# A mixture-of-experts layer's row table: from one packed table to a region per expert

## The chip, the cores and the metric

One Trainium2 chip, one of its cores. The metric is the device time of one launch in microseconds. The core's engines are called PE (TensorE), DVE (VectorE), ACT (ScalarE), POOL (GpSimd) and SP (SyncE). SP and ACT issue plain DMAs; POOL issues the indirect ones, whose row addresses come from memory.

## The reference, cut to what matters

```python
x = L0_attn_x                                  # (8, 512, 256) float32: 4096 tokens
x = x + _L0_attn_ref(_layernorm(x), ...)       # only the first 16 rows of each of the 8 batches
                                               # attend (eff = 16); for all others only the bias ob is added
x = x + _L0_ffn_ref(_layernorm(x), ...)

# _L0_ffn_ref, for each token: E = 32 experts, 4 of them chosen
scores = sigmoid(tokens @ router_weight.T)     # groups of 8 experts; the best 2 of 4 groups stay,
topk_idx, topk_w = ...                         # of these the 4 best; weights scaled to a sum of 2.5
hidden_vals = silu(tokens @ gate_w[e].T) * (tokens @ up_w[e].T)     # I = 128
expert_out = hidden_vals @ down_w[e].T
mixed = sum over the 4 chosen of topk_w * expert_out
return mixed + shared                          # shared: two more experts, for every token
```

So the 128 rows that attend have their second-layer input only after three rounds of attention; the other 3968 rows have theirs at once.

## The kernel before

The tokens are 32 tiles of 128 rows. Tile 0 holds the attending rows (16 of each batch), tiles 1 to 31 all others. Everything is float32. Each engine's program is written out by hand, with semaphores between them; no scheduler moves anything.

**Stage 1, tiles 1 to 31 (0 to 57 us).** DVE adds `ob` and takes the statistics (`statistics`, groups of tiles in `GROUPS_OF_TILES`), ACT normalises (L572), PE turns the tile (L736), ACT keeps the turned tile (L577), PE makes the 32 logits of the router (L742), ACT the sigmoid (L581) in two halves.

**Stage 2, routing on DVE (41 to 89 us).** `route` (L1069 to L1122) finds the four experts of each token for one half of the tiles, two matmuls (L760, L767) count pairs per expert, and DVE makes from the counts of **all** tiles the place of each (token, expert) pair in one packed table of 128-row slots, `slots_dram`, in which each expert's rows begin where the expert before it ends (L1234 to L1267). The table is first filled with blank rows by four DMAs from SP (L398), 160 tiles of 128 rows.

**Stage 3, attention and the shared experts (88 to 220 us).** `ATT_STEPS` = 23 small steps alternate PE and DVE (`after_dve` and `from_pe`; ACT does some). Between them, by the list `UNITS_AT`, stand 48 units of the shared experts: 16 gate, 16 up and 16 down; 38 of them within the 23 steps, 10 behind. PE does its units of a step before it waits for DVE's part of that step. In the same time POOL scatters the normalised rows of tiles 1 to 31 to the table: four indirect DMAs of 128 rows for each tile (L535), each followed by a one-column memset on POOL (L538). ACT writes the rows that are scattered (`stage`, L598 and L600) in a ring of four tiles, and waits in `stage(n)` until tile n - 4 has landed. `STAGE_AT` says at which step each `stage(n)` stands, `ADD_AT` where DVE adds the shared result. Behind step 22, tile 0 is normalised, turned and routed (`route_parts(0, 1, 3)`).

**Stage 4, tile 0 through all experts (220 to 263 us).** `PLAN` holds 32 "dense" steps: the 128 rows of tile 0 go through every expert, weighted by `w0`, and PE sums in PSUM (L961).

**Stage 5, the table's tiles (263 to 483 us).** 134 "expert" steps (`FIXED`). SP loads 128 rows of the table (L425, ring of 16), PE turns them (L922), gate and up (L946), silu on ACT (L689), product on DVE (L1439), PE turns (L952), DVE copies (L1445), down (L970), ACT copies (L698), POOL scatters the 128 results to `pairs_dram` by an indirect DMA (L542). Parts behind `FIXED` run only if the table is longer (`used_parts`).

**Stage 6 (483 to 549 us).** For each of the tiles 1 to 31 SP loads the four result rows per token (L457), DVE adds them with their weights (L1477), SP stores.

For the inputs here the routing fills 133 tiles of the table with the pairs of tiles 1 to 31, and 136 with those of all 32 tiles, each expert rounded up to whole tiles (counted from the reference's choice of experts).

## Time and profile before

| | us |
|---|---|
| median of 3 runs | 551.88 (550.71 to 553.16) |
| the profiled execution | 550.75 |
| its span, first to last instruction | 549.0 |
| TensorE clock granted, mean of the span | 0.936 |
| first attention step on PE | 88.27 |
| dense steps begin | 219.74 |
| first expert step on a tile of the table | 264.88 |
| last expert step | 481.16 |

Times in the rows are microseconds from the span's start. A row of the timeline names the engine, the line of the kernel, the operation, what it writes and reads, and in brackets how long the engine had been idle and what released it. The clock is given as a share of full speed (2.4 GHz); half of it is the lower level, 1.2 GHz.

### The profile page before, as it was taken

The page shows a single profiled execution, that of the slowest core. Times are in us where ns is not written, and L with a number is a line of the kernel's source. Part 1 is how long each engine was busy: PE and PEld are TensorE (multiplying, and loading weights), DVE is VectorE, ACT ScalarE, POOL GpSimd, SP SyncE. Part 2 cuts the span into 40 slices and gives each one's busy share as a digit, 9 for nine tenths or more (in the row PEclk, how much of TensorE's full clock was granted, in tenths as well). Part 3 has the DMA queues.
Part 4 walks back from the last instruction along what each step waited for, and adds up shares of the span by engine and source line. Part 5 has one row for each costly group of instructions (what it writes and reads, how often), then busy time and mean ns, then how long its engine had stood idle before and what let it go on. Part 6 is the DMA issues. An engine that isn't in the chain of part 4 may idle for free.

```text
span 549.0 us, 8776 instructions
## 1 busy us (share of the span) xinstructions
PE 418.3 (76%) x2118; PEld 325.6 (59%) x2119; DVE 280.3 (51%) x997; ACT 240.5 (44%) x625; POOL 287.9 (52%) x421
## 2 busy tenths in 40 slices
PE   0699236898896976999999999999999999920000
PEld 0699114555453543888888888888888888810000
DVE  4967785764553434343366633223232322308997
ACT  0687501427644552422455555555555555510000
POOL 6430028886888888760166565656656565630000
PEclk9999998999998998999999999999999999985555
DMA  7999999532232373935055555455454454339996
GB/s 178 274 419 417 418 423 398 149 107 77 106 106 98 106 266 124 366 98 155 11 168 157 162 152 149 153 162 157 145 169 153 154 172 139 105 106 410 369 402 241
DMA packets 42549, 111.48 MB, mean 203 GB/s; under 512 B 7929, under 2 KB 25468, under 8 KB 38272
## 3 DMA queue, kind: packets, MB, share of 16 engines
q1 hardware_dynamic: 29824, 78.24, 41.5%
q0 software_dynamic: 12384, 32.59, 17.1%
q8 instruction: 23, 0.38, 0.3%
q14 instruction: 30, 0.25, 0.2%
q10 hardware_dynamic: 288, 0.03, 0.0%
HBM read 53.01 MB, written 59.13 MB: 204 GB/s over the span
## 4 chain that ended last, share of the span: by engine, by line
PE 53%; DVE 9%; ACT 2%; DMA 1%; issue 1%; SPq 0%; POOL 0%; POOLq 0%; ACTq 0%; DVEq 0%
PE two_banks L946 26%; PE two_banks L970 11%; DVE x_sb L1477 9%; PE two_banks L922 5%; PE two_banks L952 3%; PE two_banks L783 3%; PE two_banks L961 3%; PE two_banks L809 2%; DMA gu_w<-pairs_dram 1%; ACT L588 0%; ACT loopb L598 0%; DMA pairs_dram<-routing,loopb 0%; ACT routing L612 0%; PE two_banks L887 0%; PE two_banks L904 0%
## 5 line engine op out<-in xcount | busy, mean ns | idle before, releaser
L542 POOL DMA_INDIRECT pairs_dram<-routing,loopb x134 | 131.8, 984 | 112.0 <-issue 80.9
L535 POOL DMA_INDIRECT slots_dram<-loopb,slot_i x124 | 121.5, 979 | 70.6 <-DVEq L1267 41.8
L946 PE MATMUL two_banks<-gu_w,routing 128*128 x536 | 137.9, 380 | 0.0
L1439 DVE TENSOR_TENSOR routing<-routing,two_banks 128x128 f32<-128x128 f32 x134 | 38.6, 288 | 135.8 <-ACT routing L689 122.9
L946 PEld LDWEIGHTS two_banks<-gu_w,routing 128*128 128x128 f32 x536 | 91.5, 190 | 7.0
L970 PE MATMUL two_banks<-dn_w,routing 128*128 x268 | 80.0, 381 | 0.0
L684 ACT ACTIVATE routing<-two_banks 128x256 f32<-128x256 f32 x134 | 51.5, 384 | 64.9 <-PE two_banks L922 64.9
L783 PE MATMUL two_banks<-gu_w,sgu_w 128*128 128x512 f32 x128 | 64.8, 644 | 11.1 <-DMA sdn_w<-in_sh_down 5.5
L689 ACT ACTIVATE routing<-two_banks 128x128 f32<-128x128 f32 x166 | 46.1, 278 | 58.7 <-PE two_banks L946 58.7
L1477 DVE SCALAR_TENSOR_TENSOR x_sb<-gu_w,wts,x_sb 128x256 f32<-128x256 f32 x124 | 49.5, 480 | 12.7 <-DMA gu_w<-pairs_dram 12.6
L698 ACT ACTIVATE routing<-two_banks 128x256 f32<-128x256 f32 x134 | 50.6, 378 | 1.4 <-PE two_banks L970 1.3
L922 PE MATMUL two_banks<-ident,loopb 128*128 128x128 f32 x268 | 51.2, 273 | 0.0
L598 ACT ACTIVATE loopb<-x_sb,shift,rstd 128x1024 f32<-128x1024 f32 x31 | 38.2, 1233 | 27.4 <-DMA slots_dram<-loopb,slot_i 27.3
L1445 DVE COPY routing<-two_banks 128x128 f32<-128x128 f32 x166 | 47.1, 284 | 0.4 <-PE two_banks L952 0.2
L970 PEld LDWEIGHTS two_banks<-dn_w,routing 128*128 128x128 f32 x268 | 40.5, 191 | 10.3 <-issue 0.2
L783 PEld LDWEIGHTS two_banks<-gu_w,sgu_w 128*128 128x128 f32 x128 | 24.6, 205 | 36.9 <-issue 23.7
L922 PEld LDWEIGHTS two_banks<-ident,loopb 128*128 128x128 f32 x268 | 37.8, 141 | 13.5 <-issue 0.2
L952 PE MATMUL two_banks<-ident,routing 128*128 128x128 f32 x166 | 45.4, 274 | 0.3
L809 PE MATMUL two_banks<-sdn_w,loopb 128*128 128x256 f32 x128 | 32.7, 400 | 11.2 <-ACT gu_w L612 7.4
L809 PEld LDWEIGHTS two_banks<-sdn_w,loopb 128*128 128x128 f32 x128 | 24.3, 198 | 19.5 <-issue 12.5
L736 PE MATMUL two_banks<-ident,gu_w 128*128 128x128 f32 x62 | 20.5, 438 | 19.4 <-ACT gu_w L572 19.4
L946 PE MATMUL two_banks<-gu_w,xnT 128*128 128x256 f32 x128 | 32.7, 379 | 0.0
(222 smaller groups left out, 476.9 us busy)
## 6 DMA issues: line engine op xcount, KB each, us to landing
slots_dram<-gu_w SPq DMA_DIRECT2D x4, 5140.0 KB, 47.4
loopb<-slots_dram SPq DMA_DIRECT2D x134, 128.5 KB, 2.5
gu_w<-pairs_dram SPq DMA_DIRECT2D x31, 512.0 KB, 6.8
gu_w<-in_gate_up SPq DMA_DIRECT2D x4, 2048.0 KB, 12.9
out<-x_sb SPq DMA_DIRECT2D x3, 1024.0 KB
dn_w<-in_down SPq DMA_DIRECT2D x1, 2304.0 KB, 9.7
pairs_dram<-routing,loopb POOLq DMA_INDIRECT x134, 2.8
slots_dram<-loopb,slot_i POOLq DMA_INDIRECT x124, 3.2
```

The source lines that it names most:

```text
L535: pool.indirect_dma_start(out=slots_dram, out_offset=bass.IndirectOffsetOnAxis(ap=slot_i[:, at:at + 1], axis=0), in_=xg[:, r, 0:ROW], in_o ...
L542: pool.indirect_dma_start(out=pairs_dram, out_offset=bass.IndirectOffsetOnAxis(ap=xg[:, u % RING, D:ROW].bitcast(I32), axis=0), in_=yb[u % ...
L684: act.activation(xT[:, j % 2], turn_ps[j % 2], ACT.Copy).then_inc(xT_ready, 1)
L698: act.activation(yb[u % OUTS], y_ps(u), ACT.Copy).then_inc(y_ready, 1)
L783: ins = pe.matmul(o, weights[:, m, c, :], xnT[:, 4 * q:4 * q + 4, c, :], start=(c == 0), stop=(c == KC - 1))
L809: ins = pe.matmul(pair_y_ps[:, i, :], pair_hid[:, m, t:t + P], sdn_w[:, m, :], start=(m == 0), stop=(m == 1))
L922: ins = pe.transpose(turn_ps[j % 2][:, c, :], xg[:, u % RING, c * P:(c + 1) * P], ident[:, :])
L946: ins = pe.matmul(bank[2 + s % 2][:, 0:2 * I], rows[:, c, :], w, start=(c == 0), stop=(c == KC - 1))
L952: pe.transpose(bank[4 + s % 2][:, 0:P], hid[:, s % 2, 0:I], ident[:, :]).then_inc(hid_turned, 1)
L970: ins = pe.matmul(y_ps(n), hidT[:, s % 2, 0:P], w, start=True, stop=True)
L1445: dve.tensor_copy(hidT[:, s % 2, 0:P], bank[4 + s % 2][:, 0:P]).then_inc(hidT_ready, 1)
L1477: ins = dve.scalar_tensor_tensor(x_sb[:, m + 1, :], load4[:, m % LOADS, k, :], wts[:, m + 1, k:k + 1], x_sb[:, m + 1, :], ALU.mult, ALU.add)
```

## The change

- **A region per expert.** The table has 4224 rows (`CAP`) for each of the 32 experts and 128 spare rows behind them. A pair's row is its expert's first row plus its rank among the expert's pairs, so it needs only the counts of the tiles before it. Ranks come from one prefix scan on DVE and two or three matmuls (`rank`) for each of three parts of the tiles (`PARTS`: 8, 8 and 15).
- **Order.** Part 0 is routed before attention begins, parts 1 and 2 in pieces inside the attention steps 0 to 9 (`ROUTE_AT`). Four `stage` calls stand among the normalisations of stage 1 (`EARLY_STAGE`). `STAGE_AT` and `ADD_AT` are made from new numbers. `UNITS_AT` puts 19 instead of 16 units into steps 0 to 9 and 19 instead of 22 behind.
- **Tile 0 goes through the table.** The 32 dense steps are gone. Its four scatters come last, then the table of expert and first row for each tile is made (`ecol`, `tables`), and stage 5 runs 137 steps. Stage 6 sums 32 tiles.
- **Blanks.** Instead of the whole table, 256 rows behind each expert's rows of tiles 1 to 31 are blanked by 32 DMAs (L384) whose address SP reads into a register; tile 0's rows are then written over them.
- **Loads.** SP's 137 loads of the table (L417) take their address from a register, four addresses at a time (`load_row`).
- **POOL.** The memset behind each row scatter is gone.

```diff
...
+CAP = TOKENS + P
+SPARE = E * CAP
+CAP_TILES = CAP // P
+USED_MOST = (PAIRS + E * (P - 1)) // P
+GROUPS_OF_TILES = [(1, 5), (5, 9), (9, 17), (17, 25), (25, 32)]
+PARTS = [(1, 9), (9, 17), (17, 32)]
+HALVES = [(0, 16), (16, 32)]
...
-FIXED = 134
+FIXED = 137
...
+UNITS_AT = [2, 2, 2, 2]
+UNITS_AT += [2, 2, 2, 3, 1, 1]
+UNITS_AT += [2, 1, 2, 2, 1, 1]
+UNITS_AT += [1, 1, 2, 2, 1, 2, 1]
...
+ROUTE_AT = {0: [(1, 0), (1, 1)], 1: [(1, 2), (1, 3)], 2: [(1, 4)], 3: [(1, 5), (1, 6)],
+            4: [(2, 0)], 5: [(2, 1)], 6: [(2, 2)], 7: [(2, 3)], 8: [(2, 4)], 9: [(2, 5), (2, 6)]}
+RANK_AT = {step + 1: part for step, pieces in ROUTE_AT.items() for part, piece in pieces if piece == 4}
+EARLY_STAGE = {14: 0, 18: 1, 22: 2, 26: 3}
+RANK_EARLY = 18
+SCATTER_US, FIRST_US, ATT_US, STEP_US = 5.2, 47.0, 62.0, 5.5
...
+    _us = FIRST_US + SCATTER_US * _n - 9.6
+    _at = max(int((_us - ATT_US) / STEP_US), 0)
+    STAGE_AT.setdefault(("att", _at) if _at < ATT_STEPS else ("tail", 0), []).append(_n)
...
-            sp.wait_ge(blank_made, 2)
-            for u in range(0, SLOT_TILES // BLOCK, BLANKS):
-                sp.dma_start(slot_blocks[:, u:u + BLANKS, :],
-                             blank[:, :, :].rearrange("p j d -> p (j d)").unsqueeze(1).to_broadcast(
-                                 [P, BLANKS, BLOCK * ROW])).then_inc(blanked, 16)
...
+            sp.dma_start(dn_w[:, 18:E], down[:, 18:E]).then_inc(dn_in[1], 16)
+            sp.wait_ge(blank_made, 2)
+            sp.dma_start(slots_dram[SPARE:SPARE + P, :], blank[:, 0, :]).then_inc(spare_made, 16)
+            sp.wait_ge(blanks_known, 1)
+            for first in range(0, E, 4):
+                _, starts = nc.values_load_multi_w_load_instructions(
+                    blank_at[0:1, first:first + 4], engines=(mybir.EngineType.SP,), min_val=0, max_val=SPARE - BLANK_ROWS,
+                    skip_runtime_bounds_check_because="a slot of an expert that is followed by P or more rows of its own")
+                for at in starts:
+                    sp.dma_start(slots_dram[bass.ds(at, BLANK_ROWS), :].rearrange("(p j) d -> p (j d)", j=2),
+                                 blank[:, :, :].rearrange("p j d -> p (j d)")).then_inc(blanked, 16)
+            sp.wait_ge(blanked, 16 * E)
...
+            def load_row(u):
+                first = u // EIDS * EIDS
+                if first not in rows_at:
+                    _, rows_at[first] = nc.values_load_multi_w_load_instructions(
+                        tables[0:1, 2 * P + first:2 * P + first + EIDS], engines=(mybir.EngineType.SP,), min_val=0,
+                        max_val=SPARE, skip_runtime_bounds_check_because="clamped to the spare rows where the table is made")
+                return rows_at[first][u % EIDS]
+
             def load_tile(u):
...
-                sp.dma_start(xg[:, u % RING, 0:ROW], slot_tiles[:, u // BLOCK, u % BLOCK, :]).then_inc(xg_in[u % RING], 16)
-
+                sp.dma_start(xg[:, u % RING, 0:ROW], slots_dram[bass.ds(load_row(u), P), :]).then_inc(xg_in[u % RING], 16)
+
+            sp.wait_ge(tables_ready, 1)
             for r in range(RING):
...
-            pool.wait_ge(blanked, 16 * (SLOT_TILES // BLOCK // BLANKS))
-            for n in range(TT - 1):
-                pool.wait_ge(slots_ready, 1 + [a <= n + 1 < b for a, b in SLOT_PARTS].index(True))
+            for n in range(TT):
+                t = (n + 1) % TT
+                if t == 0:
+                    pool.wait_ge(blanked, 16 * E)
+                    pool.wait_ge(slots_ready, len(PARTS) + 1)
+                else:
+                    pool.wait_ge(slots_ready, 1 + [a <= t < b for a, b in PARTS].index(True))
                 pool.wait_ge(staged, 2 * n + 2)
                 for k in range(TOPK):
                     r = n % MOVES * TOPK + k
-                    at = (n + 1) * TOPK + k
+                    at = t * TOPK + k
                     pool.indirect_dma_start(out=slots_dram,
                                             out_offset=bass.IndirectOffsetOnAxis(ap=slot_i[:, at:at + 1], axis=0),
                                             in_=xg[:, r, 0:ROW], in_offset=None).then_inc(moved[r], 16)
-                    pool.memset(pause[:, n * TOPK + k:n * TOPK + k + 1], 0.0)
...
+                if n in EARLY_STAGE:
+                    stage(EARLY_STAGE[n])
...
-            scores(*HALVES[1], logit_ps[1])
-            for n in range(MOVES):
-                stage(n)
+            scores(*PARTS[2], logit_ps[2][:, 0:15 * E])
             load_table(ACT.Silu)
-            act.wait_ge(slots_ready, 1)
...
-            for n in STAGE_AT.get(("route", 0), []):
+            units(BEFORE_LOGITS, len(UNITS))
+            for n in STAGE_AT.get(("tail", 0), []):
                 stage(n)
-            units(BEFORE_LOGITS, len(UNITS))
...
+            stage(TT - 1)
...
+            def rank(part):
+                pe.wait_ge(hot_ready, part + 1)
+                if part < len(PARTS):
+                    a, b = PARTS[part]
+                    pe.matmul(rank_ps[part], ones_b[:, :], prefix[part][:, :, 0:b - a].rearrange("p e t -> p t e"), start=True,
+                              stop=False, skip_group_check=True)
+                    ins = pe.matmul(rank_ps[part], lower[:, :], hot[part][:, :, 1:].rearrange("p e t -> p t e"), start=False,
+                                    stop=True, skip_group_check=True)
+                    if part == len(PARTS) - 1:
+                        ins = pe.matmul(total_ps, ones_b[:, :], prefix[part][:, :, b - a], start=True, stop=True,
+                                        skip_group_check=True)
+                else:
+                    pe.matmul(rank_ps[part], lower[:, :], hot_0[:, :], start=True, stop=True, skip_group_check=True)
+                    ins = pe.matmul(total_ps, ones_b[:, :], hot_0[:, :], start=True, stop=True, skip_group_check=True)
+                ins.then_inc(rank_done, 1)
...
+                if n == RANK_EARLY:
+                    pe.wait_ge(consts_made, N_CONSTS)
+                    rank(0)
...
-            pe.wait_ge(tables_ready, 1)
             turn(TT - 1)
             units(BEFORE_TURN, BEFORE_LOGITS)
-            logits(TT - 1, xnT_0, logit_0_ps)
-            units(BEFORE_LOGITS, len(UNITS))
...
+            logits(TT - 1, logit_0_ps)
+            units(BEFORE_LOGITS, BEFORE_LOGITS + 4)
+            rank(len(PARTS))
+            units(BEFORE_LOGITS + 4, len(UNITS))
+            pe.wait_ge(ecol_ready, 1)
+            for c in range(4):
+                ins = pe.matmul(table_ps[:, c * P:(c + 1) * P], ecol[:, c:c + 1], ident[:, :], start=True, stop=True)
+            ins.then_inc(table_turned, 1)
+            pe.wait_ge(tables_ready, 1)
...
+                    if k:
+                        dve.tensor_copy(hot[k][:, :, 0], prefix[k - 1][:, :, spans[k - 1] // E - 1])
+                    seq(dve.tensor_scalar(hot[k][:, :, 1:], masked.rearrange("p t e -> p e t"), -HUGE, None, ALU.is_equal))
+                    dve.tensor_tensor_scan(prefix[k].rearrange("p e t -> p (e t)"), resets[k].rearrange("p e t -> p (e t)"),
+                                           hot[k].rearrange("p e t -> p (e t)"), 0.0, ALU.mult, ALU.add
+                                           ).then_inc(hot_ready, 1)
...
+            def slots_of(a, b, nth, counts, start, chosen_of):
+
+                n = b - a
+                placed_ab = placed3[:, a:b]
+                dve.wait_ge(rank_done, nth)
+                seq(dve.tensor_tensor(placed_ab, counts.rearrange("p (t e) -> p t e", e=E),
+                                      start[:, :].unsqueeze(1).to_broadcast([P, n, E]), ALU.add))
+                seq(dve.tensor_tensor(placed_ab, chosen_of, placed_ab, ALU.mult))
+                yield
+                for t in range(a, b):
+                    ins = dve.max(top8[:, t, :], placed3[:, t, :])
+                seq(ins)
+                dve.tensor_scalar(slot_i[:, a * TOPK:b * TOPK].rearrange("p (t k) -> p t k", k=TOPK), top8[:, a:b, 0:TOPK],
+                                  -1.0, None, ALU.add).then_inc(slots_ready, 1)
+                yield
...
+            def know_blanks():
+
+                seq(dve.tensor_tensor(next_slot[:, :], total_ps, first_slot[:, :], ALU.add))
+                dve.tensor_scalar(blank_at[0:1, :], next_slot[0:1, :], -1.0, None, ALU.add).then_inc(blanks_known, 1)
...
+                    for part, piece in ROUTE_AT.get(step, []):
+                        next_of(part)
+                        if (part, piece) == (2, 5):
+                            know_blanks()
...
```

PE, from tile 0's turning to the first tiles of the table. Before (L736 turns tile 0, L783 and L809 are units of the shared experts, L946 on `xnT` is a dense step):

```order
L736 MATMUL two_banks<-ident,at_d 128x128 x2
L809 MATMUL two_banks<-sdn_w,loopb 128x256 x8
L742 MATMUL two_banks<-rt_w,xnT 128x32 x2
L783 MATMUL two_banks<-gu_w,sgu_w 128x512 x8
L809 MATMUL two_banks<-sdn_w,loopb 128x256 x8
L946 MATMUL two_banks<-gu_w,xnT 128x256 x4
L952 MATMUL two_banks<-ident,routing 128x128
```

The changed kernel (L899 turns the table's columns, L907 turns a tile of the table):

```order
L723 MATMUL two_banks<-ident,at_d 128x128 x2
L793 MATMUL two_banks<-sdn_w,loopb 128x256 x8
L729 MATMUL two_banks<-rt_w,gu_w 128x32 x2
L768 MATMUL two_banks<-gu_w,sgu_w 128x512 x8
L749 MATMUL two_banks<-routing,lower 128x32
L750 MATMUL two_banks<-routing,ones_b 128x32
L793 MATMUL two_banks<-sdn_w,loopb 128x256 x8
L899 MATMUL two_banks<-ident,ecol 1x128 x4
L948 TENSOR_LOAD tables
L907 MATMUL two_banks<-ident,loopb 128x128 x4
```

The ranks of tile 0 stand between its units, and a tile of the table follows the units directly; 32 dense steps stood there.

DVE, at attention step 1 to 2. Before (L1143 is the product of a unit, L1279 and L1284 are attention):

```order
L1143 TENSOR_TENSOR loopb<-loopb,two_banks 128x512
L1279 COPY routing<-two_banks 128x512
L1281 CAST eids<-two_banks 1x256
L1284 TENSOR_SCALAR routing<-two_banks,col_sb 128x128
```

The changed kernel (L1156, L1245 and L1248 are the same three; L1070 to L1088 choose the experts of part 1):

```order
L1245 COPY routing<-two_banks 128x512
L1156 TENSOR_TENSOR loopb<-loopb,two_banks 128x512
L1070 TENSOR_TENSOR small<-gu_w 128x32
...
L1084 TENSOR_SCALAR small<-small 128x32
L1085 TENSOR_TENSOR routing<-routing,small 128x256
L1088 MAX top<-routing 128x8 x8
L1248 TENSOR_SCALAR routing<-two_banks,col_sb 128x128
```

Routing now stands between two attention operations of DVE, in each of the steps 0 to 9.

SP, the loads of the table. Before (L425 loads a tile):

```order
L418 DMA gu_w<-in_gate_up 128x4096 x2
L425 DMA loopb<-slots_dram 128x257 x17
L434 DMA out<-x_sb 8x16x256
L425 DMA loopb<-slots_dram 128x257 x117
L445 TENSOR_LOAD used
```

The changed kernel (L407 reads four addresses into registers, L417 loads a tile):

```order
L400 DMA gu_w<-in_gate_up 128x4096 x2
L407 TENSOR_LOAD tables
L417 ISA
L417 DMA loopb<-slots_dram 128x257
L417 ISA
L417 DMA loopb<-slots_dram 128x257
L417 ISA
L417 DMA loopb<-slots_dram 128x257
L417 ISA
L417 DMA loopb<-slots_dram 128x257
L407 TENSOR_LOAD tables
```

Each load has one register instruction of its own ahead of it, and every fourth a read of memory.

## Rows read from the trace of the kernel before

**Rows 1.** Stages: length, busy PE, PEld, DVE, ACT, POOL, clock, DMA share, GB/s.
```profile
88.30:195.10 106.80, 91.43 (x436) 53.99 (x436) 56.90 (x158) 52.04 (x86) 88.75 (x162) 0.97 0.36 127
195.10:219.90 24.80, 17.33 (x55) 10.27 (x56) 7.90 (x39) 10.98 (x19) 20.23 (x38) 0.93 0.63 210
219.90:263.40 43.50, 43.39 (x216) 36.57 (x215) 18.54 (x65) 13.71 (x40) 18.89 (x36) 1.00 0.59 192
263.40:481.30 217.90, 217.90 (x1206) 184.04 (x1205) 81.53 (x303) 124.36 (x398) 126.91 (x129) 1.00 0.47 145
```
**Rows 2.** Timeline of PE: the first dense steps, the first and last expert step.
```profile
219.74 1.89 PE L946 MATMUL two_banks<-gu_w,xnT 128*128 128x256 f32 x8
...
264.88 1.03 PE L946 MATMUL two_banks<-gu_w,routing 128*128 x4
...
481.16 1.03 PE L946 MATMUL two_banks<-gu_w,routing 128*128 x4
```
**Rows 3.** Timeline of DVE and PE: one half's routing, and attention's first step.
```profile
40.68 0.66 DVE L1076 TENSOR_TENSOR routing<-routing,row_sb 128x480 f32<-128x480 f32 x1
...
51.29 0.41 DVE L1122 TENSOR_SCALAR routing<-routing 128x480 bf16<-128x480 f32 x1
...
88.27 0.66 PE L826 MATMUL two_banks<-ident,routing 128*128 128x128 f32 x4 [3.85 <-DVEq L1269]
```
**Rows 4.** Timeline of ACT: two calls of `stage`, behind stage 1's last operation.
```profile
57.51 1.23 ACT L598 ACTIVATE loopb<-x_sb,shift,rstd 128x1024 f32<-128x1024 f32 x1
...
58.74 1.23 ACT L598 ACTIVATE loopb<-x_sb,shift,rstd 128x1024 f32<-128x1024 f32 x1
```
**Rows 5.** Timeline of PE: a gate or up unit (x4) at full clock, and two after idling.
```profile
95.97 1.88 PE L783 MATMUL two_banks<-gu_w,sgu_w 128*128 128x512 f32 x4
...
208.82 5.40 PE L783 MATMUL two_banks<-gu_w,sgu_w 128*128 128x512 f32 x8 [4.24 <-ACT loopb L609]
```
**Rows 6.** Attention's first part, in the columns of rows 1.
```profile
88.30:132.00 43.70, 38.44 (x184) 23.03 (x185) 24.71 (x69) 20.49 (x34) 34.70 (x65) 0.96 0.47 161
```
**Rows 7.** Timeline of DVE and POOL: scatters with the memset, and without.
```profile
77.89 0.19 DVE L1266 SCALAR_TENSOR_TENSOR slot_i<-slot_p,slot_i 128x32 int32<-128x32 int32 x1
...
79.02 1.20 POOL L535 DMA_INDIRECT slots_dram<-loopb,slot_i  x1 [41.80 <-DVEq L1267]
...
81.79 0.96 POOL L535 DMA_INDIRECT slots_dram<-loopb,slot_i  x1 [0.19 <-issue]
...
83.05 0.96 POOL L535 DMA_INDIRECT slots_dram<-loopb,slot_i  x1 [0.18 <-issue]
...
485.26 0.98 POOL L542 DMA_INDIRECT pairs_dram<-routing,loopb  x1 [0.30 <-issue]
486.55 0.99 POOL L542 DMA_INDIRECT pairs_dram<-routing,loopb  x1 [0.30 <-issue]
```
**Rows 8.** The row scatters' line: who waited (us, times), min/median/max time to landing.
```profile
  ACT loopb L598: 27.3, 7
...
DMA to landing us min/median/max: 2.5/3.2/11.9
```
**Rows 9.** While DVE routes: POOL busy in row scatters, then DVE busy.
```profile
79.00:89.00 10.00, 7.84 (x8) 1.00 1.02 425
...
79.00:89.00 10.00, 8.99 (x44) 1.00 1.02 425
```
**Rows 10.** DMA issues of the page: KB each, median us to landing.
```profile
loopb<-slots_dram SPq DMA_DIRECT2D x134, 128.5 KB, 2.5
...
gu_w<-in_gate_up SPq DMA_DIRECT2D x4, 2048.0 KB, 12.9
```
**Rows 11.** SP's waits ahead of the loads: us in total, times, longest.
```profile
SPq L424 <- DMA pairs_dram<-routing,loopb: 166.1, 111, 20.2
```
**Rows 12.** The chain at the end: SP's register read, then the last stage's sums.
```profile
488.95 0.48 SPq L445
...
496.61 47.60 DVE x_sb L1477 x120
```

614 lines of the change are left out of this document (256 added, 358 removed).

## The prediction

> **What bounds the kernel now.** I read the stages first. [rows 1]: over stage 5 (263 to 481 us) PE is busy for all of its 217.9 us, in the 43.5 us of the dense steps for 43.4. So there PE alone sets the time, and POOL, ACT and DVE have room. In attention (106.8 us) PE is busy 91.4 and DVE 56.9: the two hand over to each other, and PE is nearly full of the shared experts' units. Before that come 88.3 us until attention's first step [rows 3]; from 40.7 us on DVE routes one half, then the other, and attention waits for it though it needs nothing of it. Second, the timeline of PE [rows 2]: dense steps from 219.74, the first step on a tile of the table at 264.88, the last at 481.16. That is 45.1 us for 32 dense steps (1.41 each) and 216.3 / 133 = 1.626 us for each step of the table. Third, the last part of the chain: DVE's sums, 120 in 47.60 us, 0.397 each [rows 12].
>
> The profiled execution took 550.75 us, 1.75 more than its span of 549.0, and 1.1 less than the median of 551.88. I sum against the span and add 2.9 at the end.
>
> **The change, part by part.** I follow one time: when the first step on a tile of the table begins, 264.9 before.
>
> *Start of attention.* Routing of parts 1 and 2 no longer stands ahead of it. On PE, stage 1 is done at about 57 (ACT's `stage` begins at 57.51 behind its last sigmoid [rows 4]). Four `stage` calls now stand inside it, 1.23 us each [rows 4]: 62. Two units at 1.88 [rows 5] come ahead of the first step: 65 to 66. DVE is earlier: it had all but routing done at 40.68 [rows 3]; routing 8 tiles costs some 8 us of the 11.0 that 15 tiles took (40.68 to 51.70), because most of its operations are short ones whose length hardly shrinks, ranks and slots 3, the last group's root by Newton steps 2: 54. So PE sets it, at **65** instead of 88.3. Bounds: 61, if ACT's gaps take in all four stages, and 69, if DVE or ACT is 4 us worse.
>
> *Length of attention.* Parts 1 and 2 now stand between DVE's attention operations of steps 0 to 9. They cost about 8 + 3 and 11 + 4 us, with the blanks' addresses 27 in all. In the first 43.7 us of attention, about those steps, DVE was busy 24.7 [rows 6], so 19 of 27 find room and 8 do not, if all room could be used. PE has 5.3 us of room there, and gets three more units (5.6 us) and the rank matmuls, 1 to 2 us; the three units are missing later, where PE is nearly full too. And ACT waited 27.3 us there for scatters to land before it could write the next ring place [rows 8]; with the scatters started some 30 us earlier against attention than now, part of this goes. I take 8 for DVE and 3 for places where both wait: 106.8 becomes **118**. Bounds: 107 if PE's units hide everything, 134 if all 27 us are serial. The new placement list counts on 5.5 us for a step, 126 in all; that is a number of the code, no measurement, and lies inside.
>
> *From tile 0's norm to the end of the units.* 24.8 us now [rows 1]. Three `stage` calls stood on ACT ahead of a gate's silu, and PE idled 4.24 us behind them [rows 5]; they go. The rank of tile 0 stands between units and needs five pieces of DVE work, about 1 us exposed: **22**. The units end at 65 + 118 + 22 = 205.
>
> *The dense steps go: 45.1 us, all on PE.* What they hid comes out, and has to be paid. Behind the last unit: ACT writes ring places for tile 30 and tile 0 (the first 1.2), POOL wakes (0.9: from 78.08 to 79.02 [rows 7]), eight scatters, landing 3.2 at the median [rows 8], SP's address read 0.5 [rows 12] and a little more, a load of the table 0.4 to issue and 2.5 to land [rows 10], PE's turn and ACT's copy 1.2. A scatter with its memset comes every 1.26 us (81.79 to 83.05). Without one, the last two of stage 5's scatters, both with their data ready, start 1.29 apart [rows 7]: 0.98 and a gap of 0.30. So the memset cost nothing, and its removal brings nothing; eight scatters are 10.2. Sum 20.4. PE idles for these, and comes back slow: two units took 5.40 us after 4.24 us of idling, where full clock gives 3.76 [rows 5]. I add 2. The gap is **22.4**, the first step on the table at 205 + 22.4 = **227.4**, 37.5 earlier. Bounds of landing: 2.5 and 11.9 [rows 8], so -1 and +9; the second half of the experts' weights is on its way at the same time (12.9 us to land [rows 10], asked for at the last up unit some 5 us before the units end), which argues for some of it but lands before it is needed.
>
> *Are the scatters there in time?* Tile 1's slots exist at about 46 to 47 us: part 0's sigmoid near 31, 8 us of choosing, PE's rank near 43, 2.3 us of slots. From 47, thirty tiles at 5.1 need until 201. ACT's writing of tile 30 comes at 205. It fits by a few us only.
>
> *Blanks.* The four large writes at the start become 32 small ones beside attention. What waited for the large ones were the loads behind them on SP's queue (`sgu_w` and `sdn_w`, which PE awaits at its first unit); now these come ahead, and are there when PE reaches its units at 62. That belongs to the start above and is no gain of its own. SP is held at the 32 writes until part 2 has its ranks; behind them stand the first half of the experts' weights, needed only at 227.
>
> *Three more steps:* 137 instead of 134 at 1.626: +4.9. *Four more sums* at 0.397: +1.6.
>
> *SP's loads by register.* Before each load SP runs a register instruction, before each fourth a memory read (0.48 [rows 12]). SP had 166.1 us of waits ahead of 111 of its loads [rows 11], 1.5 us of room for each. What a load by register costs no row shows. Between 0 and 1.5 us it is hidden by a ring of 16 loads; I take 0.
>
> The Trainium skill, page "DMA: Bandwidth & Descriptors", section "Latency and other measured facts", gives about 600 ns as the floor of such a memory read. By it the four-tile group costs SP 0.6 us where the row's 0.48 stands, and the sum stays.
>
> **Sum:** 549.0 - 37.5 + 4.9 + 1.6 = 518.0; with 2.9 around it, **521 us**.
>
> **Rivals.**
>
> *Routing is serial with attention.* Every piece delays DVE's answer, and PE's next unit waits for it too. For it: DVE's step and PE's step hand over strictly. Against it: PE's units of a step are done before PE waits. Attention takes 134, 16 more: 537.
>
> *Attention hides it all.* The stretch is 0 and ACT's waits shrink: 11 less, 510.
>
> *The scatters become the path, and it is slower.* Scatters now run beside routing, and beside all of attention. In the 10 us where they already did, DVE was busy 8.99 and eight scatters took 7.84, the first with its 1.20 included [rows 9], so I see no slowing. But if each of the 128 took 0.33 us longer because of DVE, and came every 1.62 instead of 1.29 us, the stream from 47 would last 207 us, to 254.4. Landing, load and turn (8.1) and the clock's 2 bring the first step to 264.5, where it was: 549 - 0.4 + 6.5 + 2.9 = **558**. It decides from about 1.33 us a scatter, where the stream ends behind ACT's last ring place, and costs 128 us for each further us; from 1.57 it eats all of the gain.
>
> The rule for such a delay is on the Trainium skill's page "SBUF — State Buffer", section "SBUF: two separate sides": a DVE operation with two SBUF inputs and a GpSimd operation that reads SBUF exclude each other for the whole instruction. By it the routing's two-input operations would hold off scatters; [rows 9] do not show it.
>
> *The change doesn't do what it says.* Scatters start at 47 but starve, because ACT, tied up in attention, writes the ring places late; the ring is four tiles, 20 us. Then more than two tiles are left at the units' end, each 5.1 us. Two more: 531, inside the forecast's range.
>
> **How the numbers follow.** Forecast 0.72 (own range 513 to 533), routing serial 0.12, all hidden 0.07, scatters the path 0.05, SP's register loads above 1.6 us each (as slow or slower) 0.02, some mixture near no change 0.02. The first three are faster: 0.91. The range of 508 to 541 takes in the serial case and the late landing. A measurement of this kernel can tell 0.5% (2.8 us) from no change.
>
> **What would show it.** Right: PE's first attention step near 65 and first step on the table near 227; the step there still 1.63; POOL's scatters 1.26 to 1.29 apart from 47 us; DVE busy over 75% in the first 50 us of attention. Wrong: PE waiting on `tables` or the first load later than 235; ACT's `stage` waiting more than 10 us for landings, or POOL for ACT; steps of stage 5 longer than 1.65, with PE waiting for SP's loads; attention over 130 us.

## Result and the profile after

The changed kernel takes 528.4 us (527.2 to 529.1, 4 runs) beside 552.5 us for the kernel before in the same runs: ratio 0.956, interval 0.952 to 0.960, so 24 us faster. The forecast was 521 in a range of 508 to 541: the direction and the range hold, the sum is 7 us too low. The profiled execution's span is 527.2 us where the sum had 518.0. Here and below, medians and ratios leave out executions in the chip's slower state, those more than 1.5% above the fastest of their kernel.

Windows of the kernel after, in the columns of [rows 1]: attention until tile 0's norm, from there to the end of the units, the gap until the first step on a tile of the table, the steps until the last one, the rest.
```profile
68.00:192.10 124.10, 94.85 (x438) 55.27 (x436) 79.81 (x306) 55.86 (x92) 92.40 (x94) 0.93 0.65 184
192.10:213.60 21.50, 16.76 (x64) 10.02 (x64) 9.06 (x53) 8.48 (x17) 9.62 (x10) 1.00 0.75 276
213.60:236.90 23.30, 1.25 (x4) 0.58 (x5) 4.42 (x9) 2.47 (x5) 10.34 (x8) 0.57 0.70 248
236.90:459.10 222.20, 222.20 (x1218) 187.43 (x1218) 81.82 (x304) 126.41 (x405) 129.83 (x132) 0.99 0.50 153
459.10:527.20 68.10, 3.08 (x13) 1.75 (x11) 52.18 (x133) 1.81 (x5) 4.92 (x5) 0.55 0.84 319
```
PE's timeline at the borders: the first two units and the first attention step (L813), the first turn of a loaded tile (L907), the first step (L921). The last one begins at 459.12.
```profile
62.27 5.89 PE L768 MATMUL two_banks<-gu_w,sgu_w 128*128 128x512 f32 x8
68.00 0.60 PE L813 MATMUL two_banks<-ident,routing 128*128 128x128 f32 x4
...
235.65 1.33 PE L907 MATMUL two_banks<-ident,loopb 128*128 128x128 f32 x4 [22.08 <-DMA loopb<-slots_dram]
236.90 2.07 PE L921 MATMUL two_banks<-gu_w,routing 128*128 x4
```
Stage by stage against [rows 1, 2, 3] and the prediction's steps:

| | before | predicted | after |
|---|---|---|---|
| first attention step | 88.3 | 65 | 68.0 |
| attention until tile 0's norm | 106.8 | 118 | 124.1 |
| norm to the end of the units | 24.8 | 22 | 21.5 |
| dense steps, or the gap in their place | 45.1 | 22.4 | 23.3 |
| first step on the table at | 264.9 | 227.4 | 236.9 |
| first to last of these steps | 216.3 | 221.2 | 222.2 |
| from the last step's start to the end | 67.8 | 69.4 | 68.1 |

So 9.5 us of the miss stand ahead of the first step, 6.1 of them in attention; the steps give 1.0 more and the end takes 1.3 back.

Attention first. PE is busy 94.85 of 124.1 us, before 91.43 of 106.8 [rows 1]: its idle time grew from 15.4 to 29.3 us, and its matmuls, as many as before, took 3.4 us more. Two waits make up most of the growth. The rows: PE ahead of a rank matmul and ahead of a down unit, then ACT's ring places around the second.
```profile
119.58 1.02 PE L741 MATMUL two_banks<-gu_w,ones_b 128*128 128x480 bf16 x1 [6.32 <-DVE gu_w L1103]
...
164.06 3.75 PE L793 MATMUL two_banks<-sdn_w,loopb 128*128 128x256 f32 x8 [9.56 <-ACT gu_w L611]
...
156.88 1.24 ACT L597 ACTIVATE loopb<-x_sb,shift,rstd 128x1024 f32<-128x1024 f32 x1 [4.38 <-DMA slots_dram<-loopb,slot_i]
162.10 1.24 ACT L597 ACTIVATE loopb<-x_sb,shift,rstd 128x1024 f32<-128x1024 f32 x1 [3.41 <-DMA slots_dram<-loopb,slot_i]
163.34 0.57 ACT L611 ACTIVATE gu_w<-two_banks 128x512 f32<-128x512 f32 x1
```
PE waited 6.32 us until DVE's routing of part 2 had its prefix sums (L1103), with attention's own matmuls (L869) queued behind the rank; another such wait, at 80.7, took 2.3. And it waited 9.56 us for ACT's copy of a down unit (L611), because ACT stood ahead of a ring place (L597) until an older scatter had landed. Before, the longest wait of the second kind was 5.14. Behind the 9.56 us PE is slow: the down unit takes 3.75 us, where most take 1.89 to 1.99, and the granted clock from 164.06 to 168.00 is 0.50.

Attention by its three iterations, the first with the steps ahead of it, the third until the norm:
```profile
68.00:111.80 43.80, 37.01 (x153) 21.82 (x152) 38.05 (x147) 17.72 (x30) 30.94 (x33) 1.00 0.27 94
111.80:144.30 32.50, 23.12 (x115) 13.69 (x114) 22.29 (x103) 15.13 (x26) 25.18 (x25) 0.89 0.66 180
144.30:192.10 47.80, 34.73 (x173) 19.76 (x171) 19.48 (x59) 23.01 (x38) 36.28 (x38) 0.89 1.00 270
```
The pieces of routing lie in the first two. All of ACT's waits for landings lie in the third: the first of them ends at 147.4.

The second place is the gap. The end of GpSimd's stream of row scatters, DVE's sums of pairs beside it, SP's queue, and the chain that ended last:
```profile
215.24 3.62 POOL L534 DMA_INDIRECT slots_dram<-loopb,slot_i  x1 [10.72 <-ACT loopb L599]
226.75 0.96 POOL L534 DMA_INDIRECT slots_dram<-loopb,slot_i  x1 [0.30 <-issue]
...
214.27 1.27 DVE L1165 TENSOR_TENSOR x_sb<-x_sb,gu_w 128x512 f32<-128x512 f32 x2
215.47 1.88 DVE L1165 TENSOR_TENSOR x_sb<-x_sb,routing 128x512 f32<-128x512 f32 x3
...
217.62 0.41 DVE L1168 TENSOR_TENSOR x_sb<-x_sb,loopb 128x256 f32<-128x256 f32 x1
...
215.62 0.80 SPq L400 DMA_DIRECT2D gu_w<-in_gate_up  x2
233.58 2.75 SPq L417 DMA_DIRECT2D loopb<-slots_dram  x5
...
226.75 6.27 DMA slots_dram<-loopb,slot_i
233.58 2.02 DMA loopb<-slots_dram
```
GpSimd has nothing to do from 204.5 to 215.2, since the last two ring places are written behind the last unit; then the first of eight scatters takes 3.62 us instead of 0.96; the last, begun at 226.75, has landed for SP at 233.58, 6.8 us later, with 4 MB of weights on their way since 215.62. All of it is about 1 us longer than the sum of 22.4.

The whole stream (minimum, median, maximum in ns, first and last start; GpSimd's own wait for ACT ahead of it; ACT's waits for it; time to landing, which was 2.5/3.2/11.9 before [rows 8]):
```profile
L534 POOL DMA_INDIRECT slots_dram<-loopb,slot_i x128: 956/960/3623, 46.7 to 226.8; - x128
  ACT loopb L599: 12.2, 6
  ACT loopb L597: 17.8, 7
DMA to landing us min/median/max: 2.5/5.0/13.1
```

### The profile page after: what moved, and what is told of

It is laid out like the page before. It is cut to its first block, busy times and chain, and to the rows that moved or that the text cites. A ratio compares the mean times of both kernels' runs of the same rounds, so it can differ in the third digit from the quotient of the medians.

```text
span 527.2 us, 8577 instructions
## 1 busy us (share of the span) xinstructions
PE 382.8 (73%) x1930; PEld 294.4 (56%) x1930; DVE 267.8 (51%) x977; ACT 235.1 (45%) x604; POOL 280.9 (53%) x307
## 4 chain that ended last, share of the span: by engine, by line
PE 52%; DVE 18%; DMA 11%; POOL 8%; issue 5%; ACT 4%; SPq 1%; DVEq 0%; POOLq 0%; ACTq 0%
PE two_banks L921 23%; PE two_banks L938 11%; DVE x_sb L1448 8%; DMA slots_dram<-loopb,slot_i 6%; PE two_banks L907 6%; POOL slots_dram L534 6%; PE two_banks L927 3%; PE two_banks L768 3%; DMA gu_w<-pairs_dram 3%; PE two_banks L729 2%; POOL rstd L481 2%; PE two_banks L723 2%; PE two_banks L793 1%; ACT loopb L597 1%; DMA x_sb<-in_x 1%
## 5 line engine op out<-in xcount | busy, mean ns | idle before, releaser
L540 POOL DMA_INDIRECT pairs_dram<-routing,loopb x137 | 134.8, 984 | 103.0 <-issue 82.8
L534 POOL DMA_INDIRECT slots_dram<-loopb,slot_i x128 | 128.7, 1006 | 65.8 <-issue 36.0
L921 PE MATMUL two_banks<-gu_w,routing 128*128 x548 | 142.9, 384 | 0.0
L921 PEld LDWEIGHTS two_banks<-gu_w,routing 128*128 128x128 f32 x548 | 94.5, 193 | 7.7 <-issue 0.3
L680 ACT ACTIVATE routing<-two_banks 128x256 f32<-128x256 f32 x137 | 52.5, 383 | 85.6 <-PE two_banks L907 85.4
L907 PE MATMUL two_banks<-ident,loopb 128*128 128x128 f32 x274 | 53.1, 276 | 22.1 <-DMA loopb<-slots_dram 22.1
L768 PE MATMUL two_banks<-gu_w,sgu_w 128*128 128x512 f32 x128 | 62.1, 622 | 0.4 <-ACT loopb L608 0.4
L907 PEld LDWEIGHTS two_banks<-ident,loopb 128*128 128x128 f32 x274 | 38.7, 142 | 36.6 <-DMA loopb<-slots_dram 22.7
L692 ACT ACTIVATE routing<-two_banks 128x256 f32<-128x256 f32 x137 | 51.8, 378 | 1.4 <-PE two_banks L938 1.3
L685 ACT ACTIVATE routing<-two_banks 128x128 f32<-128x128 f32 x137 | 38.0, 277 | 31.5 <-PE two_banks L921 31.5
L597 ACT ACTIVATE loopb<-x_sb,shift,rstd 128x1024 f32<-128x1024 f32 x32 | 39.4, 1232 | 17.8 <-DMA slots_dram<-loopb,slot_i 17.8
L938 PEld LDWEIGHTS two_banks<-dn_w,routing 128*128 128x128 f32 x274 | 41.4, 191 | 10.5 <-issue 0.2
L793 PE MATMUL two_banks<-sdn_w,loopb 128*128 128x256 f32 x128 | 33.6, 408 | 14.3 <-ACT gu_w L611 11.4
L1425 DVE COPY routing<-two_banks 128x128 f32<-128x128 f32 x137 | 38.8, 283 | 0.4 <-PE two_banks L927 0.2
L768 PEld LDWEIGHTS two_banks<-gu_w,sgu_w 128*128 128x128 f32 x128 | 24.4, 201 | 24.5 <-issue 22.8
L927 PE MATMUL two_banks<-ident,routing 128*128 128x128 f32 x137 | 37.4, 273 | 0.1
L793 PEld LDWEIGHTS two_banks<-sdn_w,loopb 128*128 128x128 f32 x128 | 24.6, 201 | 21.5 <-issue 16.0
L729 PEld LDWEIGHTS two_banks<-rt_w,gu_w 128*128 128x128 f32 x128 | 30.7, 329 | 0.6 <-issue 0.5
## 6 DMA issues: line engine op xcount, KB each, us to landing
gu_w<-in_gate_up SPq DMA_DIRECT2D x4, 2048.0 KB, 11.7
```

The lines of the kernel that those rows point to most:

```text
L534: pool.indirect_dma_start(out=slots_dram, out_offset=bass.IndirectOffsetOnAxis(ap=slot_i[:, at:at + 1], axis=0), in_=xg[:, r, 0:ROW], in_o ...
L540: pool.indirect_dma_start(out=pairs_dram, out_offset=bass.IndirectOffsetOnAxis(ap=xg[:, u % RING, D:ROW].bitcast(I32), axis=0), in_=yb[u % ...
L597: act.activation(xg[:, r:r + TOPK, 0:D], x_sb[:, t, :].unsqueeze(1).to_broadcast([P, TOPK, D]), ACT.Identity, bias=shift[:, t:t + 1], scal ...
L680: act.activation(xT[:, u % 2], turn_ps[u % 2], ACT.Copy).then_inc(xT_ready, 1)
L692: act.activation(yb[u % OUTS], y_ps(u), ACT.Copy).then_inc(y_ready, 1)
L768: ins = pe.matmul(o, weights[:, m, c, :], xnT[:, 4 * q:4 * q + 4, c, :], start=(c == 0), stop=(c == KC - 1))
```

## Experiments

Times are medians; ratios stand against the kernel before in the same runs. Attention's 120.5 us in the expectations runs to PE's last attention matmul; to tile 0's norm, as in the table, it is 124.1. "First step" is the first on a tile of the table. Row times are read from the profiled execution of each.

**The memset back.**
```diff
                                             in_=xg[:, r, 0:ROW], in_offset=None).then_inc(moved[r], 16)
+                    pool.memset(pause[:, n * TOPK + k:n * TOPK + k + 1], 0.0)
```


> The changed kernel with the small GpSimd memset back behind each of the 128 row scatters, nothing else. Theory (the memset stands in a gap that is there anyway): row scatters still start 1.26 to 1.27 us apart, the first step on the table stays within 1 us of 236.9 us, the time within 1.5 us of the changed kernel's 528.4. Rival (the stream of scatters is now nearly without a break from 46.7 to 204.5 us, so each further operation on GpSimd lengthens it): a period above 1.35 us, the stream ends past 215 us, and the time is above 534.

529.1 us, ratio 0.957 (0.955 to 0.960). GpSimd's timeline, the memset of a scatter that began at 201.27, and the next scatter:
```profile
202.22 0.12 POOL L538 MEMSET pause<- 128x1 bf16 x1
202.53 0.96 POOL L535 DMA_INDIRECT slots_dram<-loopb,slot_i  x1 [0.19 <-issue]
```
The period is 1.26, as without it (idle 0.30 there, 0.19 and the memset's 0.12 here). Removing it brought nothing, as the prediction said; the rival falls.

**The end: when the last ring places are written.**
```diff
-            units(BEFORE_TURN, BEFORE_LOGITS)
+            units(BEFORE_TURN, BEFORE_TURN + 1)
+            for n in STAGE_AT.get(("tail", 0), []):
+                stage(n)
+            units(BEFORE_TURN + 1, BEFORE_LOGITS)
...
-            units(BEFORE_LOGITS, len(UNITS))
-            for n in STAGE_AT.get(("tail", 0), []):
-                stage(n)
-            stage(TT - 1)
+            units(BEFORE_LOGITS, BEFORE_LOGITS + 4)
+            stage(TT - 1)
+            units(BEFORE_LOGITS + 4, len(UNITS))
```


> The changed kernel with the last two ring places (tile 30 and tile 0) written by ACT between the last units instead of behind all of them. Theory A (GpSimd's 10.7 us without work before the last eight scatters is the wait for ACT, and lies on the path): the eight scatters follow the others without a break, the last starts near 214 instead of 226.8, the first step on the table comes at 222 to 226 instead of 236.9, and the time is 10 to 14 us below 528.4, so 514 to 518. Theory B (the end of the second half of the experts' weights, asked for at 215.6 and some 17 us on their way, is just behind): the step comes no earlier than 232, and the time is 523 or more.

523.5 us, 0.948 (0.946 to 0.950). SP's timeline, the weights and the first loads of the table:
```profile
217.23 0.80 SPq L400 DMA_DIRECT2D gu_w<-in_gate_up  x2
219.08 12.10 SPq L417 DMA_DIRECT2D loopb<-slots_dram  x16
```
The first half of theory A is right: the last scatter starts at 215.1, 11.7 earlier, and has landed at 219.1. But the loads that SP issues then take up to 11.3 us to land, behind 4 MB of weights asked for at 217.23, PE waits 15.22 us for the first of them, and the first step comes at 231.7: nearly B's number (232), in B's range of times.

**The end: DVE's sums ahead of tile 0's routing.**
```diff
+ADD_AT["gap", 0] = [j for j in ADD_AT["tail", 0] if j < SHARED - 2]
+ADD_AT["tail", 0] = [SHARED - 2, SHARED - 1]
...
             units(UNITS_FROM[-1], BEFORE_LOGITS)
+            add_pairs("gap", 0)
```


> The changed kernel with four of DVE's six last sums of shared pairs (10 to 13) done between attention and tile 0's routing, where DVE is idle for 7 us, instead of behind the table. SP's load of the second half of the experts' weights waits for one of them. Theory A (the last scatters land late, 6.8 us, because these weights are on their way beside them, and the first of them takes 3.62 instead of 0.96 us because DVE adds with two SBUF inputs while it wants to read): weights asked for near 207 instead of 215.6, the first of the last eight scatters at 2 us or less, the last landing in 3 to 4 us, the first step on the table at 231 to 233, the time 523 to 525. Theory B (neither is on the path): no change, 527 to 530.

522.5 us, 0.946 (0.944 to 0.949), 1 us less than with the places early, which the intervals don't tell apart. SP asks for the weights, GpSimd starts the first of the last eight scatters, PE turns the first tile:
```profile
204.83 0.89 SPq L402 DMA_DIRECT2D gu_w<-in_gate_up  x2
...
213.73 0.96 POOL L536 DMA_INDIRECT slots_dram<-loopb,slot_i  x1 [8.41 <-ACT loopb L601]
...
228.09 1.18 PE L909 MATMUL two_banks<-ident,loopb 128*128 128x128 f32 x4 [16.04 <-DMA loopb<-slots_dram]
```
Weights at 204.8, the scatter at 0.96, SP past the last scatter 3.4 us after its start (222.58 to 225.95), the first step at 229.35, 7.6 earlier: theory A, with a little more than it asked for. The edit takes both of A's causes away at once, the sums beside the scatter and the late weights, so it doesn't part them.

**Both, and both with rows of four.** The second kernel has as its further edit:
```diff
...
-                    sp.dma_start(slots_dram[bass.ds(at, BLANK_ROWS), :].rearrange("(p j) d -> p (j d)", j=2),
-                                 blank[:, :, :].rearrange("p j d -> p (j d)")).then_inc(blanked, 16)
+                    sp.dma_start(slots_dram[bass.ds(at, BLANK_ROWS), :].rearrange("(p j) d -> p (j d)", j=4),
+                                 blank[0:64, :, :].rearrange("p j d -> p (j d)")).then_inc(blanked, 16)
```


> The changed kernel with both edits of the two runs on its end: ring places 30 and 31 written between the last units, and four of the last sums of pairs done before tile 0's routing. Each of the two alone gave 5 to 6 us. Theory A (they hinder each other's gain: the early places left PE waiting for the weights ahead of the tile loads, the early sums left GpSimd waiting for ACT; together nothing of either is left): weights asked for near 207, landed by 220, the last scatter starts near 214 and has landed by 219, the first step on the table at 221 to 224, the time 511 to 516. Theory B (the gains are of the same wait and don't add up): first step at 228 or later, the time 520 or more.

> As the kernel with both end edits, and the blanks written from 64 partitions with four rows (4,112 bytes) each instead of 128 with two (2,056 bytes): the same rows and bytes with half the pieces. Theory A (the pieces' number sets what a blank costs): the 32 writes are through by 155 us instead of 183, ACT's waits for landings fall by half, attention is 4 us or more shorter, and the time 4 us or more below that of the kernel with both end edits. Theory B (the bytes set it): within 1.5 us of that kernel, and the DMA engines as full as before until near 180.

522.8 us (0.943, 0.938 to 0.948) and 522.1 us (0.944, 0.938 to 0.951). The gains don't add up. Both, GpSimd's last scatter and SP's queue:
```profile
215.58 2.66 POOL L536 DMA_INDIRECT slots_dram<-loopb,slot_i  x1 [0.30 <-issue]
...
208.13 0.82 SPq L402 DMA_DIRECT2D gu_w<-in_gate_up  x2
228.78 9.06 SPq L419 DMA_DIRECT2D loopb<-slots_dram  x16
```
The last scatter starts at 215.6, 7 us before that of the kernel with the sums alone, and yet SP passes it only at 228.8, 10.5 us after its end. Now the weights, asked for at 208.1, lie beside it. So theory A's 219 fell: it had taken the weights' and the scatters' times one by one. The scatter itself took 2.66 us instead of 0.96. Larger pieces for the blanks changed nothing (theory B).

**Weights in two pieces**, with both end edits.
```diff
...
+            sp.wait_ge(up_done, SHARED // 2)
+            sp.wait_ge(pair_added, SHARED // 2)
+            second(2)
             sp.wait_ge(norm_ready, len(GROUPS_OF_TILES) + 1)
             sp.dma_start(dn_w[:, 0:18], down[:, 0:18]).then_inc(dn_in[0], 16)
             sp.wait_ge(up_done, SHARED)
             sp.wait_ge(pair_added, KEPT_IN_XNT)
...
+            second(3)
```


> As the kernel with both end edits, and the second half of the experts' gate and up weights (4 MB) asked for in two pieces: the 2 MB that lie where the first 16 tiles of xnT were, as soon as those are used up (behind the first half, near 187 us), the other 2 MB as now (near 208). Theory A (in that kernel the last scatter, issued by 218.2, landed only at 228.8 because 4 MB of weights stood beside it, and in the one with early places alone the tile loads took 11 us behind the same 4 MB; so 4 MB behind the last up unit are what sets the gap): the last scatter lands by 222, the first step on the table comes at 222 to 225 instead of 232.1, the time 513 to 517. Theory B (the DMA engines then are full from 184 on, scatters land later, ACT's ring places come later, and the gain is given back): the first step at 229 or later, the time 520 or more.

523.0 us, 0.945 (0.939 to 0.951): theory B. Windows as above; the last two numbers are the DMA engines' share and GB/s.
```profile
128.00:188.00 60.00, 42.89 (x214) 24.88 (x213) 27.31 (x82) 29.68 (x49) 45.69 (x48) 0.91 1.01 242
188.00:226.00 38.00, 24.76 (x85) 14.09 (x83) 18.39 (x80) 13.61 (x23) 21.05 (x22) 0.90 0.96 363
226.00:228.00 2.00, 0.00 (x0) 0.00 (x0) 0.00 (x0) 0.00 (x0) 0.00 (x0) 0.50 0.00 0
```
The first step comes at 231.2. The DMA engines are full from 128 to 226 us and idle for the 2 us until the last scatter counts as landed (SP's first load at 227.8); from 68 to 127 they were busy for 0.27. The order of the transfers moved; their sum did not.

**The blanks cut, alone and with these edits.**
```diff
...
-                    sp.dma_start(slots_dram[bass.ds(at, BLANK_ROWS), :].rearrange("(p j) d -> p (j d)", j=2),
-                                 blank[:, :, :].rearrange("p j d -> p (j d)")).then_inc(blanked, 16)
+                    n = BLANKS_OF[e]
+                    if n:
+                        sp.dma_start(slots_dram[bass.ds(at, n), :].rearrange("(p j) d -> p (j d)", j=2),
+                                     blank[0:n // 2, :, :].rearrange("p j d -> p (j d)")).then_inc(blanked, 16)
```


> The changed kernel with the blanks cut to what these inputs need: 18 of the 32 experts, 32 to 192 rows each instead of 256, 1,824 rows instead of 8,192. The other blank rows are left out (on other inputs some would be missing). Theory A (the 32 blank writes, 8.4 MB, keep the DMA engines full from 127 to 183 us, so row scatters land after 8.9 instead of 2.8 us, ACT waits for them 13 us in the third iteration, and PE 9.6 behind ACT): scatters land in 3 to 4 us at the median, ACT's waits fall below 6 us, attention is 7 to 10 us shorter than 120.5, PE's wait of 9.6 us is gone. The last eight scatters start that much earlier too, since they wait for ACT behind the units: the time is 519 to 523. Theory B (ACT's places come as early as GpSimd's stream lets them, blanks or not): ACT's waits stay above 12 us and the time above 526.

> As the kernel with both end edits and the weights in two pieces, and the blanks cut to the 1,824 rows that these inputs need; the other 6,368 blank rows are left out. In that kernel the last scatter was issued by 218.0 and landed at 227.8, with the DMA engines without a break in work from 127 to 226 us: 8.4 MB of blanks, 10.8 MB of weights, some 9 MB of scatters. Theory A (after the end edits the DMA engines' bytes are the bound of the gap): the first half of the weights is asked for near 147 instead of 188, the engines have room before 208, the last scatter lands by 221, the first step on the table comes at 220 to 224 instead of 231.2, the time 512 to 516. Theory B (scatters land late near the end for another reason, and the blanks cost nothing here either, as they cost nothing alone): first step at 229 or later, time 520 or more.

Alone: 527.9 us, 0.953 (0.948 to 0.958), no change. The scatters' landing; PE at the place of the wait of 9.56 us; a tile's last scatter, and ACT where it waits for that tile to land; the window from SP's next weights on:
```profile
DMA to landing us min/median/max: 2.4/3.2/10.1
...
164.61 3.75 PE L797 MATMUL two_banks<-sdn_w,loopb 128*128 128x256 f32 x8 [10.31 <-ACT gu_w L615]
...
153.09 0.96 POOL L538 DMA_INDIRECT slots_dram<-loopb,slot_i  x1 [0.30 <-issue]
...
162.65 1.24 ACT L601 ACTIVATE loopb<-x_sb,shift,rstd 128x1024 f32<-128x1024 f32 x1 [5.10 <-DMA slots_dram<-loopb,slot_i]
...
146.60:164.00 17.40, 7.63 (x49) 4.71 (x45) 7.48 (x27) 5.45 (x11) 13.45 (x14) 0.83 0.95 342
```
Landing falls to 3.2 us at the median, and from 127 to 183 us the DMA share from 1.01 to 0.65, but not where ACT waits. Without the large blanks SP asks for the first half of the weights, 4 MB, at 146.6 instead of 183.2, and from there to 164 the DMA engines are as good as full again (0.95). ACT's wait that ends at 162.65 is for a tile whose last scatter ended at 154.05, 8.6 us before. In the changed kernel that is 8.4 us at the same place, and 1.7 to 2.7 at ACT's waits in the third iteration of the kernel before. So ACT's waits still make 12.4 us, PE waits 10.31, and the time is theory B's; but the premise of theory A, quick landing, was not there, and which of the two causes PE's wait stays open.

With the other edits: 591.3 us beside 631.0 for the kernel before, on a chip where both kernels were slower; 0.938 (0.931 to 0.945), a ratio that was counted as unclear. Attention takes 167 us, the first half of the weights is asked for at 188.8 and not at 147, and GpSimd's scatters waited 52.3 us for ACT. Neither theory's premise was there. Whether fewer bytes would shorten the gap is therefore open: the windows of the kernel with the weights in two pieces speak for it, no run shows it.

**Ring places one step later.**
```diff
-    _us = FIRST_US + SCATTER_US * _n - 9.6
+    _us = FIRST_US + SCATTER_US * _n - 4.1
     _at = max(int((_us - ATT_US) / STEP_US), 0)
+    if _n < TT - 2:
+        _at = min(_at, ATT_STEPS - 1)
```


> The changed kernel with each of ACT's writes of ring places in attention set one step (5.5 us of the placement's own count) later, the last of them still inside attention. Theory A (ACT stands 13 us in the third iteration waiting for scatters to land that the 32 blanks' writes hold up, and PE waits 9.6 us behind ACT): ACT's waits for landings fall from 17.8 us to below 6, attention is 6 to 10 us shorter than its 120.5, and GpSimd still has no idle time above 2 us in the stream, so the units end earlier, but the stream of scatters, which ends near 204.5, then decides: the time is 2 to 6 us below 528.4. Theory B (the later writes starve GpSimd): the stream ends 4 us or more later and the time is above 530.

530.0 us, 0.958 (0.955 to 0.962). PE's longest wait for ACT fell from 9.56 to 6.85, but ACT's waits for landings rose to 20.3, GpSimd waited 14.2 for ACT, and the stream's first 30 tiles ended 4.3 us later (208.8 against 204.5). Theory A fell. Of theory B the stream's later end came out; the time can't be told from the changed kernel's 528.4.

**Routing ahead of attention again.** `ROUTE_AT` is empty, DVE runs all pieces of parts 1 and 2 ahead of attention, PE both rank matmuls in its first step; the lists of ring places and sums are made anew from a start of attention at 80 us and 4.8 us a step.

> The changed kernel with the routing of parts 1 and 2 and the blanks' addresses ahead of attention again, as one block, and the placement's counts moved to it (attention from 80 us, 4.8 us a step); all else as changed. Theory A (by the sum of the prediction: interleaving costs 11 us of attention and saves some 20 at its start): the first attention step at 80 to 86 us instead of 68, attention 105 to 112 us long instead of 120.5, the units end 4 to 8 us later, the time 532 to 537. Theory B (routing inside attention is serial all the same, so nothing is gained by it): attention 98 to 103 us, the time within 2 us of 528.4. The blanks' writes come earlier too, beside the first iteration.

536.8 us, 0.970 (0.965 to 0.975). Attention's three iterations, cut as in the result, and PE's longest wait for ACT in them:
```profile
92.50:132.90 40.40, 37.52 (x149) 22.51 (x149) 23.14 (x61) 13.96 (x24) 24.36 (x25) 0.95 1.05 233
132.90:163.50 30.60, 23.37 (x113) 14.28 (x114) 12.80 (x32) 15.50 (x27) 21.63 (x22) 0.89 0.88 281
163.50:199.40 35.90, 32.20 (x173) 18.25 (x171) 19.58 (x60) 21.26 (x36) 27.36 (x29) 1.00 0.30 104
...
155.69 3.75 PE L792 MATMUL two_banks<-sdn_w,loopb 128*128 128x256 f32 x8 [4.36 <-ACT gu_w L610]
```
Together they take 106.9 us, as attention did in the kernel before (106.8), and begin at 92.5, 24.5 us later than in the changed kernel; to the last attention matmul it is 103.2, a little outside both theories. Theory A's total came out (532 to 537). Routing inside attention makes the start 24.5 us earlier and attention 17.2 longer, so it is worth 7 us, not the 20 that its earlier start suggests.

But not all of the 17.2 us is routing's. The three iterations are 3.4, 1.9 and 11.9 us shorter here than in the changed kernel. Most of the difference lies in the third, which holds no routing in either kernel: in the changed one PE waits there 9.56 us behind ACT's ring places, here no more than 4.36, and that in the second.

**Rank one step later.**
```diff
-RANK_AT = {step + 1: part
+RANK_AT = {step + 2: part
```


> The changed kernel with PE's rank matmuls of parts 1 and 2 one attention step later in PE's order, nothing else. PE waited 2.3 and 6.3 us in front of them for DVE's piece of routing, and attention's own matmuls stood behind. Theory A (it is PE's order that makes these pieces serial, not DVE's time): both waits are gone or below 1 us, attention is 4 to 7 us shorter than 120.5, and, since the last ring places are written behind the last unit, the first step on the table comes 3 to 6 us earlier than 236.9: the time 523 to 526. Theory B (DVE is the one that is full there, and PE only waits elsewhere): attention within 1.5 us of 120.5, the time 527 to 530.

527.7 us, 0.954 (0.948 to 0.960): no gain that can be told, though the first step on the table comes at 234.5, 2.4 us earlier. PE at the same place, and attention's window:
```profile
112.86 1.39 PE L869 MATMUL two_banks<-routing 128*32 128x64 f32 x32 [0.40 <-ACT routing L658]
119.37 1.02 PE L741 MATMUL two_banks<-gu_w,ones_b 128*128 128x480 bf16 x1 [2.75 <-DVE routing L1335]
...
67.40:190.30 122.90, 96.54 (x438) 56.09 (x436) 80.36 (x307) 57.47 (x96) 93.30 (x94) 0.93 0.67 185
```
Attention's matmuls (L869) are done at 114 instead of 124, and still DVE, which has routing from 111 to 118.7, comes to them only then. Attention is 122.9, 1.2 shorter (119.2 against 120.5 to its last matmul), and a wait of 9.09 us behind ACT's ring places stays. DVE's time is the cost, mostly, not PE's order: theory B.

**Sums early and rank late together.** The last run leaves nothing out. Its expectation takes attention to be 2 us shorter by the late rank; by the rows above it was 1.3.

> The changed kernel with two edits that leave nothing out: four of the last sums of pairs before tile 0's routing (alone 522.5 us), and PE's rank matmuls one attention step later (alone it made attention 2 us shorter and the first step 2.4 us earlier). Theory A (both shorten what stands before the last ring places, one behind the other): the first step on the table at 226 to 228 instead of 236.9, the time 519 to 521.5. Theory B (the DMA engines' bytes set the gap as soon as it is shortened): the first step stays at 229, the time at 522 to 524.

598.0 us beside 631.0, 0.946 (0.940 to 0.952), on the same chip as the kernel with the blanks cut and the other edits. By ratio it equals the kernel with the sums alone. Its scatters waited 71.8 us for ACT, where the changed kernel's waited 12.2, so it decides between neither theory. Five kernels of the study that leave nothing out can't be told apart by their intervals: sums early (522.5 us, 0.946), ring places early (523.5, 0.948), both (522.8, 0.943), both with larger pieces for the blanks (522.1, 0.944) and both with the weights in two pieces (523.0, 0.945). They are some 1% below the changed kernel and 5.2 to 5.7% below the one before; the sums alone are the smallest edit.

## Why the prediction was right, and where 9 us went

**Right in mechanism and size.** Dense steps gone for a gap of about 23 (22.4 forecast). Norm to the units' end 21.5 (22): ACT no longer stands three places long ahead of a gate, and PE's 4.24 us of idling [rows 5] are gone. Steps on the table: 222.2 us over 136 intervals, 1.634 each, and PE never waits for a load once it has begun, so SP's register loads are hidden as said. They have rows of their own now: 37 and 29 ns beside 333 for the issue.
```profile
L417 SPq FUSED_REGOPS  x137: 37/37/42, 233.4 to 443.6; - x137
L417 SPq MOVE loopb<-slots_dram x137: 29/29/37, 233.5 to 443.7; - x137
L417 SPq DMA_DIRECT2D loopb<-slots_dram x137: 332/333/1173, 233.6 to 443.8; - x137
```
The memset: nothing, shown by its return.

**Start of attention, 65 against 68.0.** The units begin at 62.27, as summed (62). The two of them take 5.7 us, where I took full clock's 1.88 each: the first matmul of 512 columns lasts 1.20 instead of 0.59 us. That is 2.0 us. Another 0.8 is rounding, since 62 and two times 1.88 make 65.8 and I went on with 65. A row for such a pair stood in front of me [rows 5], two units in 5.40 us after idling, and I used it only for the gap. DVE had no part in it.

**Attention, 118 against 124.1: the step that failed.** I let 19 of routing's 27 us find room in DVE's idle time and exposed 8, added 3 for places where both wait, and let ACT's waits shrink. The kernel with routing ahead shows 17.2 us in place of these 11. By its iterations 5.3 of them lie in the two that hold routing, 11.9 in the third. Its second iteration has a wait behind ACT of its own, 4.36 us, and a slow unit behind it (3.75 where 1.97 is usual). An estimate from these rows, with both taken out of it, gives routing 8.0 there and 3.4 in the first, 11.4 in all. So routing exposed some 5 to 11 us, no more than the sum had for it. The term that was mis-sized is the other one, ACT's ring places ahead of a copy that PE needs.

I had written that part of ACT's 27.3 us of waits for landings [rows 8] would go. They fell to 17.8, but a longer one lay in front of a copy for PE (9.56 against 5.14); "more than 10 us" stood among the signs of a wrong prediction, and it is what was seen. Whether it is the late landing or the place in ACT's order that makes this wait is open, since no run took it away: 10.31 us with the blanks cut, 6.85 with the places one step later, 9.09 with the rank later.

For routing itself, busy shares say how much room there is, not that it is in the right place. In the 43.8 us of the first iteration DVE is busy 38.05, 87%, more than the 75% named as a sign, and PE waited 2.26 us for a piece of routing. In the second iteration DVE was busy for only 22.29 of 32.5 us, and there PE waited 6.32.

**The gap, 22.4 against 23.3, right by errors that cancel.** The eight scatters took 12.5 us to the end of the last, not 10.2, and that one had landed 5.3 us after its end (6.27 from its start in the chain), not 3.2. Against that, the 2 us for PE's slow return came to 1 us and lie in the steps' 222.2. The first scatter began 1.6 us behind the units, not 2.1, since ACT wrote its place beside PE's table matmuls. SP's address read and load took 2.6, not 3.7; the read alone is 0.30 at the median of 35, less than both figures that the prediction has for it. Two causes of the rival "the scatters become the path" were thus real, each small. The first is contention with DVE: of the 128 scatters 17 took over 0.98 us, the first of all among them, 128.7 us busy in all where 128 at 0.96 make 122.9. The second is late landing while the weights are on their way. A pair for the first, DVE and GpSimd:
```profile
118.21 1.23 DVE L1103 TENSOR_TENSOR_SCAN gu_w<-gu_w 128x512 bf16<-128x512 bf16 x1
...
118.60 1.60 POOL L534 DMA_INDIRECT slots_dram<-loopb,slot_i  x1 [0.30 <-issue]
```
The scan ends at 119.44, the scatter 0.76 later. Behind the units the sums held a scatter from 215.24 until the last of them ended at 218.03, and it ended 0.83 later. That agrees with the rule of the Trainium skill, page "SBUF — State Buffer", section "SBUF: two separate sides", that a DVE operation with two SBUF inputs keeps a GpSimd operation that reads SBUF out for its whole length; here it is kept out for a whole run of them. In total it is 0.05 us a scatter, against 0.33 in the rival's sum and the 0.28 (1.57 less 1.29) at which it would have eaten the gain.

**In time by a few us.** The stream from 46.7 was to be through 30 tiles at 201; it was at 204.5, with DVE's slots late by 3.7 us and the contention's share in it. That was the margin, and it decides what comes next: 32 tiles of 5.2 us from 46.7 end at 213, and landing, load and turn make 5.8 more. So, as an estimate from these rows, no shortening of attention or units brings the first step below some 219, or 214 if nothing at all delays the stream (32 times 4 scatters at 1.26), as long as the row scatters go one by one.

**The rivals.** Routing serial (134, 537 us): attention lies between the two, at 124, nearer to the forecast. Hides it all: no. The change slower: no. Starving scatters: ACT waited for the stream, not the stream for ACT, except for the last eight.

## What to carry to other kernels

Work that moves into another chain's idle time is exposed by where that time lies, not by how much of it there is: look at each gap beside the piece that shall fill it. And before a difference between two placements is put down to the work that moved, split the stretch: here 11.9 of 17.2 us lay in an iteration that held none of it. When a stage that hid transfers goes, add the bytes that are now under way together in the gap, since each edit here that moved one of them alone gave 5 to 6 us, and two together no more than one. And an operation that waits for a slow stream holds up the copies that stand behind it on its engine; but no run shows a better place for it here, since one step later for all gave PE 2.7 us and cost the stream 4.3.

## What the hardware showed that I had not expected

A row scatter of 128 rows lands 2.4 to 2.5 us after its issue at the least, and up to 18.1 us with full DMA engines (in the kernel with the weights in two pieces). With 4 MB of weights asked for 17.8, 11.1 and 7.5 us before the last scatter began, SP passed it 3.4, 6.8 and 13.2 us after its start (sums early, changed kernel, both end edits). With half of the 4 MB asked for 20 us earlier it still was 10.8. A tile load behind 4 MB took 11.3 us where 2.2 is the median. That the weights are the cause is argued from these rows; no run left them out. A scatter that meets a run of DVE additions with two SBUF inputs waits for the end of the run, not of one addition (3.62 us against 0.96). PE had no idle time ahead of the first two units, and the granted clock reads 1.00 there, yet they took 5.7 us where two units take 3.6 later. The router's matmuls of stage 1 ahead of them are slow too, four in 0.90 us where four take 0.53 behind attention.
